# Two attentions on one core: attention two's query and key terms folded from SBUF to SBUF, norm and finish steps moved

## The chip, the core and the metric

The kernel runs on one core of a Trainium2 chip. The metric is the device time of one execution in microseconds; the profiled execution also has a span, from its first to its last instruction. Engines: TensorE (PE, with PEld for its weight loads), VectorE (DVE), ScalarE (ACT), GpSimd (POOL), and SyncE (SP), which here only issues transfers.

## The reference

x is (4, 16, 16, 256), that is four images of 256 tokens with 256 channels.

```
x = x + attention_one(group_norm(x))     # 8 heads of 16, relative bias, per image 8 x 256 x 256 scores
x = x + attention_two(group_norm(x))     # chunks of 64 tokens attend to their own and the previous chunk
attention_two: q, k, v = split(flat @ w_qkv.T)       # 16 heads of 16
               scores[h, l, m] = (q . k) * scale, over 128 keys; the first chunk has only its own 64
               out = softmax(scores) v, then @ w_out.T
group_norm: 32 groups of 8 channels, over all tokens of an image
```

All of it is float32. The kernel splits each float32 operand into a high float32r part and the low rest, and multiplies high by high, low by high and high by low.

## The kernel before

The work is eight units: units 0 to 3 are attention one of the four images, units 4 to 7 attention two of them (b = unit - 4). Each unit has eight blocks, and the whole is one row of steps t = 0 to 75 (`STEPS`), written out by hand for every engine: step t makes the scores of block t (unit t // 8), and the rest of the work is hung on steps by offsets from the unit's first block. `due(t, when, units)` is true for unit i at t = 8i + `when`. Each engine runs its own program in order and waits on semaphores, so where a step stands decides what it is queued behind.

In step t TensorE makes the scores of block t (`scores_b`, L590, in attention two: four matmuls of 96 rows), then transposes block t - 4 into the bank `z` (`shifted`, L600 and L609). VectorE takes the row maxima (L962, L958 in attention one) and subtracts them (L969; in attention one GpSimd, L362) into SB. ScalarE takes the exponential PT of the transposed block (`probabilities`, L1197). Scores of a block wait for the subtraction of two blocks before, transposes for that of their own block (four before) and for the PT of two before them.

Attention two, for each unit, with the offsets of before:

- XT (-14): TensorE transposes the image's X1 into bank F (L529), VectorE takes its statistics (L920, L925). Group mean (GM, -13): L538, which waits for the statistics and for bank G, that is for Qst (L881) or for ScalarE's copy VB (L1156) of the unit before. Group variance (GV, -12): L541, then VectorE's small steps, GpSimd's power (L376), and in the step after ScalarE's XTh and XT (L1133, two activations each) and after that GpSimd's XTl (L370).
- Queries and keys (QK, -9): L556, 24 matmuls; 8 on XTh and 8 more on XTh for the second bank once XT is out of it, then 8 on XTl. ScalarE copies the high parts to QHL and KHL (L1140, L1145), in the step after VectorE makes the low parts (L891). QHL and KHL are [128, 2 (high, low), 512].
- Values (V, -7): L567, which waits for VectorE's query terms; in the step after ScalarE copies them to VB (L1156), then GpSimd spreads them.
- Query and key terms: the 128 partitions of QHL are four pairs of heads by 32 rows. `scores_b` wants them as 96 partitions: 32 rows by three terms (high, low, high for queries; high, high, low for keys), with the four pairs side by side, in Q3 and K3. SP brings them there through DRAM: `put_terms` (L290) four stores of 128 KB for queries and four for keys, then `get_terms` waits for their landing and loads 512 KB into 64 partitions (L295) and 256 KB into 32 (L296). ScalarE masks the queries into QP (`pair_queries`, L1188, two activations at each even step, two steps ahead). All this stands on SP ahead of the stores of y (L316).
- Finish, per half of a unit (`FINISH`): the values matmuls (pv: 10 and 13, L679), ScalarE's copy OS (L1204, same step), the transposes t1 (12 and 15, L699), VectorE's reciprocal RC (L978) and ON (L986), the transposes t2 (14 and 17, L706), ScalarE's OT (L1212), the output product (16 and 19, L716), and in the step after VectorE's Y with the residual (L1001). The values matmuls of a half write the bank that the output product of the same half of the unit before used, so they wait for that Y.

Attention one has its own offsets (`TIMES_A`): L479 and ScalarE's XRh and VectorE's XRl, keys L494, value transposes L501, queries L485. VectorE copies the values out of bank G to VA (`value_rows`, L912) in the step after their transposes, behind that step's row maxima, and L485, which writes bank G, waits for it.

The weights of attention two are transposed by TensorE (L733) at steps 4, 5, 7 and 9, for queries, keys, values and output; ScalarE copies them to WTh (L1103), and VectorE makes WTl (L904). In steps 4 and 5 the same engines centre and scale the first images.

## Time and profile before

| | us |
|---|---|
| median of three runs | 173.7 |
| the three runs | 172.42, 173.70, 179.64 |
| the profiled execution, its own time | 175.27 |
| its span | 173.4 |
| TensorE busy in it | 151.1 |
| mean granted TensorE clock in it | 0.98 of 2.4 GHz |

The profiled execution is one execution; what is read from its rows is compared with its own time, 175.27 us, of which 1.9 us lie outside its span. In the rows, "idle before <- X" and "A <- B" give the time that an engine waited and what released it. L numbers are lines of the kernel before.

### The profile page before, as it was taken

Reading aid. Unit: us, or ns where it says so; the run is one execution under the profiler, and the core shown is the slowest. Engines: PE = TensorE matmul, PEld = TensorE weight load, DVE = VectorE, ACT = ScalarE, POOL = GpSimd, SP = SyncE. Lnnn points to the kernel's source line nnn. Section 1 sums busy time; section 2 is a strip of 40 time slices with the busy share of each in tenths; the row PEclk is TensorE's granted clock in tenths of the full one; section 3 lists DMA queues with packets and bytes.
Section 4 is the critical chain, followed back from the end, with each engine's and each line's share of the span. In section 5 each row is a group of like instructions: output and inputs, shape, how many; then the busy total and the mean of one; then the engine's idle time right before and its main releaser. Section 6 shows DMA issues by size and latency. Waiting matters only on the chain.

```text
span 173.4 us, 4284 instructions
## 1 busy us (share of the span) xinstructions
PE 151.1 (87%) x1582; PEld 130.9 (75%) x1582; DVE 111.1 (64%) x326; ACT 107.9 (62%) x218; POOL 53.0 (31%) x106
## 2 busy tenths in 40 slices
PE   7989769849989879999999798999999869989872
PEld 7568649737778578988797678988989758879751
DVE  1544776774366586277629887799687983898220
ACT  1427516857558457946795769775986774856520
POOL 0302540859946225762781122012200200000000
PEclk9999879999999999999999999999999996999999
DMA  6409900000000000049804990199309860100111
GB/s 184 138 4 275 325 6 4 0 0 0 6 2 0 4 0 2 0 121 242 246 4 104 233 266 6 32 243 240 102 5 259 206 202 0 34 14 17 34 55 42
DMA packets 8564, 15.84 MB, mean 91 GB/s; under 512 B 1208, under 2 KB 5688, under 8 KB 7776
## 3 DMA queue, kind: packets, MB, share of 16 engines
q1 hardware_dynamic: 7984, 15.22, 31.8%
q10 hardware_dynamic: 560, 0.35, 0.8%
q8 instruction: 13, 0.21, 0.5%
q14 instruction: 7, 0.06, 0.1%
HBM read 10.31 MB, written 5.26 MB: 90 GB/s over the span
## 4 chain that ended last, share of the span: by engine, by line
PE 64%; DVE 14%; DMA 6%; issue 6%; ACT 5%; POOL 2%; ACTq 1%; SPq 0%; DVEq 0%
PE bank L556 7%; PE bank L590 7%; PE bank L578 6%; PE bank L609 6%; PE bank L669 5%; PE bank L600 4%; PE bank L679 4%; PE bank L716 4%; PE bank L567 4%; DMA K<-k_terms 3%; PE bank L479 3%; DMA PT<-buckets 3%; DVE NM L962 2%; PE bank L712 2%; DVE SB L958 2%
## 5 line engine op out<-in xcount | busy, mean ns | idle before, releaser
L1197 ACT ACTIVATE PT<-bank 128x512 f32<-128x512 f32 x64 | 38.3, 598 | 23.0 <-PE bank L609 12.4
L958 DVE CUSTOM_DVE_ANT_0 SB<-bank,Tk 128x256 f32<-128x256 f32 x64 | 24.4, 420 | 20.6 <-PE bank L578 20.5
L362 POOL TENSOR_SCALAR SB<-SB,NM 128x256 f32<-128x256 f32 x64 | 29.9, 482 | 12.1 <-DVE NM L958 11.7
L962 DVE TENSOR_REDUCE NM<-bank 128x4 f32<-128x512 f32 x32 | 21.9, 685 | 12.7 <-PE bank L590 12.4
L590 PE MATMUL bank<-K,QP 96*128 96x128 f32 x128 | 21.8, 294 | 1.7 <-DMA K<-k_terms 1.7
L969 DVE TENSOR_TENSOR SB<-bank,NM 128x512 f32<-128x512 f32 x32 | 22.1, 692 | 1.1
L578 PE MATMUL bank<-KH,QM 128*128 128x256 f32 x64 | 20.6, 343 | 2.1 <-ACT QM L1177 2.1
L1188 ACT ACTIVATE QP<-Q,con 96x512 fp32r<-96x512 f32 x32 | 21.2, 713 | 0.0
L590 PEld LDWEIGHTS bank<-K,QP 96*128 96x128 f32 x128 | 17.8, 197 | 3.7 <-DMA K<-k_terms 2.0
L609 PE MATMUL bank<-con,SB 128*128 128x128 f32 x128 | 20.4, 283 | 0.0
L600 PE MATMUL bank<-con,SB 128*128 128x128 f32 x128 | 19.3, 273 | 0.0
L578 PE MATMUL bank<-KL,QM 128*128 128x256 f32 x64 | 17.3, 291 | 0.0
L578 PEld LDWEIGHTS bank<-KH,QM 128*128 128x128 f32 x64 | 12.6, 197 | 5.4 <-issue 4.9
L1177 ACT ACTIVATE QM<-Qst,con 128x256 fp32r<-128x256 f32 x32 | 16.0, 505 | 0.5 <-DVE Qst L881 0.5
L600 PEld LDWEIGHTS bank<-con,SB 128*128 128x128 f32 x128 | 14.6, 140 | 0.0
L609 PEld LDWEIGHTS bank<-con,SB 128*128 128x128 f32 x128 | 13.9, 143 | 0.2
L1204 ACT ACTIVATE OS<-bank 128x256 f32<-128x256 f32 (+1 forms) x16 | 7.8, 488 | 8.2 <-PE bank L669 5.3
L578 PEld LDWEIGHTS bank<-KL,QM 128*128 128x128 f32 x64 | 12.8, 199 | 0.2
L385 POOL COPY VB<-VB 64x256 f32<-64x256 f32 x4 | 1.6, 389 | 29.7 <-ACT VB L1156 29.7
L679 PE MATMUL bank<-PT,VB 128*32 128x64 f32 x512 | 8.8, 220 | 2.0 <-DVE Y L1001 2.0
L679 PEld LDWEIGHTS bank<-PT,VB 128*32 128x32 f32 x512 | 7.6, 110 | 3.5 <-issue 3.5
L716 PE MATMUL bank<-WoT,OT 128*128 128x256 f32 x32 | 9.3, 416 | 0.5 <-ACT OT L1212 0.5
(142 smaller groups left out, 269.7 us busy)
## 6 DMA issues: line engine op xcount, KB each, us to landing
q_terms<-WQK SPq DMA_DIRECT2D x16, 128.0 KB, 2.3
k_terms<-KHL SPq DMA_DIRECT2D x16, 128.0 KB, 2.4
Q<-q_terms SPq DMA_DIRECT2D x4, 512.0 KB, 5.4
K<-k_terms SPq DMA_DIRECT2D x4, 512.0 KB, 5.2
Tk<-bias_rows SPq DMA_DIRECT2D x4, 384.0 KB, 4.8
X<-x SPq DMA_DIRECT2D x4, 256.0 KB, 4.2
Q<-q_terms SPq DMA_DIRECT2D x4, 256.0 KB, 5.8
K<-k_terms SPq DMA_DIRECT2D x4, 256.0 KB, 6.1
```

What stands on the lines that cost most here:

```text
L362: last = nc.gpsimd.tensor_scalar(rows_of, rows_of, -1.0, NM[:, i % 2, 2 * u + nt:2 * u + nt + 1], ALU.mult, ALU.add)
L578: last = nc.tensor.matmul(s[:, nt * CH:(nt + 1) * CH], queries[:, nt * P:(nt + 1) * P], keys[:, i % 2, u // 4, :], start=(nt == 0 and keys ...
L590: last = nc.tensor.matmul(bank[S_BANK + u % 2][:, a * P:(a + 1) * P], QP[0:ROWS, c % QRING, a, g].rearrange("p v n -> p (v n)"), window, s ...
L600: last = nc.tensor.transpose(z[:, s * CH + nt * P:s * CH + (nt + 1) * P], below[:, nt * CH + s * P:nt * CH + (s + 1) * P], ident)
L609: last = nc.tensor.transpose(z[:, a * P:(a + 1) * P], below[:, a * P:(a + 1) * P], ident)
L679: last = nc.tensor.matmul(o[32 * hh:32 * hh + 32, col:col + CHUNK], VB[:, (i - BATCH) % 3, 2 * half + c2, h, :], PT[:, 4 * half + 2 * c2 + ...
L716: last = nc.tensor.matmul(o[:, 0:CH], OT[:, half, g, :], WoT[:, g, :], start=(g == 0), stop=(g == 1))
L958: last = V.tensor_tensor_reduce(SB[:, idx % SRING, nt * CH:(nt + 1) * CH], half, Tk[:, u, nt * P:nt * P + CH], 1.0, LOWEST, ALU.add, ALU.m ...
L962: V.tensor_reduce(NM[:, i % 2, 4 * u:4 * u + 4], s[:].rearrange("p (h m) -> p h m", h=4), AX.X, ALU.max).then_inc(max_ready, 1)
L969: V.tensor_tensor(SB[:, idx % SRING, :].rearrange("p (h m) -> p h m", h=4), bank[S_BANK + u % 2][:].rearrange("p (h m) -> p h m", h=4), NM ...
L1188: last = A.activation(QP[0:ROWS, c % QRING, :, :, v, :].rearrange("p a g n -> p (a g) n"), Q3[0:ROWS, b % 2, :, :, c * CHUNK:(c + 1) * CHU ...
L1197: A.activation(PT[:, u, :], bank[Z_BANK + u % 2][:], ACT.Exp, scale=-SCALE if is_a(i) else SCALE).then_inc(p_ready, 1)
```

## The change

It has five parts.

1. Terms: the DRAM tensors q_terms and k_terms and the semaphores q_written and k_written are gone. `fold_terms` takes each of the three terms of queries and keys from 128 partitions of QHL or KHL to 32 partitions of Q3 or K3 in one transfer of 256 KB, six a unit. Source partition 4r + a goes to target partition r, place a. ScalarE waits for q_loaded and k_loaded before it writes QHL and KHL again.
2. Weights: so that source partition 4r + a holds row r of pair a, the query and key weights are written in that order of columns: for n < 2 ScalarE's WTh and VectorE's WTl are written by two instructions each (one for each k), whose elements lie four apart.
3. Norm and projection steps of attention two: GM -13 to -12, GV -12 to -11, QK -9 to -8, V -7 to -6, with what follows them on the other engines; XT stays at -14.
4. Finish of attention two: t1, t2 and output product a step earlier for units 4 to 6; t1 and t2 a step earlier for unit 7.
5. VectorE's copy VA of attention one: in the step of its transposes, behind the query and key terms, instead of in the step after, ahead of them.

```diff
-        q_terms = nc.dram_tensor("q_terms", (BATCH, 2, GRP, PAIRS, 2 * TOK), F32, kind="Internal").ap()
-        k_terms = nc.dram_tensor("k_terms", (BATCH, 2, GRP, PAIRS, 2 * TOK), F32, kind="Internal").ap()
         rows = nc.dram_tensor("bias_rows", (HA, NDIAG), F32, kind="Internal").ap()
...
         fills, dve_fills = sem("fills"), sem("dve_fills")
-        q_written, k_written, q_loaded, k_loaded = (sem(n) for n in ("q_written", "k_written", "q_loaded", "k_loaded"))
+        q_loaded, k_loaded = sem("q_loaded"), sem("k_loaded")
         spread_ready = sem("spread_ready")
...
+        def pair_columns(w, n, k):
+            return w[:, k, n * CH:(n + 1) * CH].rearrange("p (g r a) -> p g a r", g=2, a=PAIRS)
+
         def grouped(t, b):
...
         TIMES_A = [(range(1, 2), (-6, -4, -5, -5)), (range(2, 3), (-5, -3, -4, -4)), (range(3, BATCH), (-9, -7, -8, -8))]
-        XT_B, GM_B, GV_B, QK_B, V_B = -14, -13, -12, -9, -7
+        XT_B, GM_B, GV_B, QK_B, V_B = -14, -12, -11, -8, -6
         FINISH = [(IN_A, (9, 12), (13, 13), (14, 14), (16, 16)),
-                  (range(BATCH, UNITS - 1), (10, 13), (12, 15), (14, 17), (16, 19)),
-                  (range(UNITS - 1, UNITS), (10, 13), (12, 15), (13, 16), (14, 17))]
+                  (range(BATCH, UNITS - 1), (10, 13), (11, 14), (13, 16), (15, 18)),
+                  (range(UNITS - 1, UNITS), (10, 13), (11, 14), (12, 15), (14, 17))]
...
-            def put_terms(b, terms, hl, ready, written):
-
-                sp.wait_ge(ready, BATCH + b + 1)
-                for a in range(PAIRS):
-                    sp.dma_start(terms[b, :, :, a, :].rearrange("s p n -> p s n"), hl[a * GRP:(a + 1) * GRP].bitcast(F32)).then_inc(written, 16)
-
-            def get_terms(b, terms, dst, both, high, written, loaded):
-
-                sp.wait_ge(written, 16 * PAIRS * (b + 1))
-                sp.dma_start(dst[GRP * both:GRP * (both + 2)], terms[b].rearrange("s p a n -> (s p) (a n)")).then_inc(loaded, 16)
-                sp.dma_start(dst[GRP * high:GRP * (high + 1)], terms[b, 0].rearrange("p a n -> p (a n)")).then_inc(loaded, 16)
+            def fold_terms(b, hl, parts, dst, loaded):
+
+                for s, part in enumerate(parts):
+                    sp.dma_start(dst[GRP * s:GRP * (s + 1), b % 2].rearrange("p a g n -> p a (g n)").bitcast(F32),
+                                 hl[:, part, :].bitcast(F32)).then_inc(loaded, 16)
...
-                n, i = b % 2, BATCH + b
-                put_terms(b, q_terms, QHL, q_ready, q_written)
-                put_terms(b, k_terms, KHL, k_ready, k_written)
+                i = BATCH + b
+                sp.wait_ge(q_ready, i + 1)
                 if b >= 2:
                     sp.wait_ge(qp_ready, NCH * (b - 1))
-                get_terms(b, q_terms, Q3[:, n].rearrange("p a g n -> p (a g n)"), 0, 2, q_written, q_loaded)
+                fold_terms(b, QHL, (0, 1, 0), Q3, q_loaded)
+                sp.wait_ge(k_ready, i + 1)
                 if b >= 2:
                     sp.wait_ge(s_done, BLK * (i - 1))
-                get_terms(b, k_terms, K3[:, n].rearrange("p a g n -> p (a g n)").bitcast(F32), 1, 0, k_written, k_loaded)
+                fold_terms(b, KHL, (0, 0, 1), K3, k_loaded)
...
                 elif u == 0:
-                    pe.wait_ge(k_loaded, 32 * (i - BATCH + 1))
+                    pe.wait_ge(k_loaded, 16 * TERMS * (i - BATCH + 1))
                 if not is_a(i) and u % 2 == 0:
...
                 src = bank[O_BANK][:].rearrange("p (k r) -> p k r", k=2)
-                V.tensor_tensor(WTl[:, :, n * CH:(n + 1) * CH], src, WTh[:, :, n * CH:(n + 1) * CH].bitcast(F32),
-                                op=ALU.subtract).then_inc(wl_ready, 1)
+                if n < 2:
+                    for k in range(CT):
+                        last = V.tensor_tensor(pair_columns(WTl, n, k), src[:, k].rearrange("p (g a r) -> p g a r", g=2, a=PAIRS),
+                                               pair_columns(WTh, n, k).bitcast(F32), op=ALU.subtract)
+                else:
+                    last = V.tensor_tensor(WTl[:, :, n * CH:(n + 1) * CH], src, WTh[:, :, n * CH:(n + 1) * CH].bitcast(F32), op=ALU.subtract)
+                last.then_inc(wl_ready, 1)
...
                     norm_x(2, t - 6)
-                for units, when in TIMES_A:
-                    for i in due(t, when[3] + 1, units):
-                        value_rows(i)
                 for step, when in enumerate((XT_B, GM_B, GV_B, GV_B + 1)):
...
                             queries_keys(i, which)
+                for units, when in TIMES_A:
+                    for i in due(t, when[3], units):
+                        value_rows(i)
                 for units, pv, t1, t2, out_step in FINISH:
...
                 src = bank[O_BANK][:].rearrange("p (k r) -> p k r", k=2)
-                dst = WTh[:, :, n * CH:(n + 1) * CH] if n < 3 else WoT[:]
-                A.activation(dst, src, ACT.Copy).then_inc(wb_ready, 1)
+                if n < 2:
+                    for k in range(CT):
+                        last = A.activation(pair_columns(WTh, n, k), src[:, k].rearrange("p (g a r) -> p g a r", g=2, a=PAIRS), ACT.Copy)
+                else:
+                    last = A.activation(WTh[:, :, n * CH:(n + 1) * CH] if n == 2 else WoT[:], src, ACT.Copy)
+                last.then_inc(wb_ready, 1)
...
                         if b:
-                            act.wait_ge(q_written, 16 * PAIRS * b)
+                            act.wait_ge(q_loaded, 16 * TERMS * b)
                         A.activation(QHL[:, 0, :], f[:], ACT.Copy).then_inc(qh_ready, 1)
...
                         if b:
-                            act.wait_ge(k_written, 16 * PAIRS * b)
+                            act.wait_ge(k_loaded, 16 * TERMS * b)
                         A.activation(KHL[:, 0, :], f[:], ACT.Copy).then_inc(kh_ready, 1)
...
                 if c == 0:
-                    act.wait_ge(q_loaded, 32 * (b + 1))
+                    act.wait_ge(q_loaded, 16 * TERMS * (b + 1))
                 if b * NCH + c >= QRING:
```

## Rows read from the trace of the kernel before

**Rows 1.** The page, part 1: busy time of each engine.

```profile
PE 151.1 (87%) x1582; PEld 130.9 (75%) x1582; DVE 111.1 (64%) x326; ACT 107.9 (62%) x218; POOL 53.0 (31%) x106
```

**Rows 2.** Windows by stage: length, busy time (instructions) of PE, PEld, DVE, ACT, POOL, clock, DMA share, GB/s.

```profile
50.00:87.00 37.00, 34.76 (x305) 30.33 (x304) 23.30 (x105) 24.68 (x54) 17.85 (x36) 1.00 0.27 72
87.00:158.00 71.00, 65.02 (x858) 59.07 (x856) 54.69 (x110) 52.01 (x101) 11.56 (x20) 0.98 0.46 120
```

**Rows 3.** Who waited for whom, PE's own: us in total, times, longest.

```profile
PE bank L679 <- DVE Y L1001: 2.0, 3, 0.8
...
PE bank L590 <- DMA K<-k_terms: 1.7, 1, 1.7
...
PE bank L485 <- DVE VA L912: 1.7, 3, 0.8
...
PE bank L538 <- ACT VB L1156: 1.6, 2, 1.2
...
PE bank L538 <- DVE Qst L881: 0.9, 1, 0.9
```

**Rows 4.** Timeline of units 6 and 7: start, us, engine, line.

```profile
128.43 0.68 DVE L891 TENSOR_TENSOR WQK<-bank,WQK 128x512 fp32r<-128x512 f32 x1
...
137.11 0.58 SPq L296 DMA_DIRECT2D K<-k_terms  x1
...
137.74 11.66 SPq L316 DMA_DIRECT2D y<-Y  x3
...
140.91 0.60 PE L699 MATMUL bank<-con,OS 128*128 128x128 f32 x4
```

**Rows 5.** The chain of waits, in order of time: start, us, what.

```profile
133.56 0.46 PE bank L609 x4
134.02 0.87 PE bank L716 x4
134.89 0.40 PE bank L590 x4
...
143.22 1.12 PE bank L590 x4
144.34 0.87 PE bank L609 x4
145.22 1.64 PE bank L716 x4
```

**Rows 6.** Windows around the wait for the key terms.

```profile
142.50:143.00 0.50, 0.00 (x0) 0.00 (x0) 0.43 (x1) 0.10 (x1) 0.00 (x0) 1.00 0.19 51
143.50:144.00 0.50, 0.50 (x4) 0.50 (x4) 0.00 (x0) 0.00 (x0) 0.00 (x0) 0.50 0.00 0
```

**Rows 7.** Windows of the stores, of the keys' load, of all unit 7's traffic.

```profile
112.00:116.00 4.00, 4.00 (x90) 3.54 (x89) 3.90 (x9) 2.13 (x5) 0.00 (x0) 1.00 0.94 249
119.50:121.00 1.50, 1.50 (x69) 1.24 (x68) 1.43 (x4) 0.64 (x2) 0.69 (x1) 1.00 0.85 224
...
129.50:142.50 13.00, 11.21 (x204) 10.31 (x202) 11.02 (x20) 9.22 (x19) 1.18 (x3) 1.00 0.86 222
```

**Rows 8.** The page, part 6: DMA issues, KB each, median us to landing.

```profile
q_terms<-WQK SPq DMA_DIRECT2D x16, 128.0 KB, 2.3
```

**Rows 9.** Timeline of the weights' step, and of two copies of 256 columns.

```profile
30.48 0.60 ACT L1103 ACTIVATE WTh<-bank 128x512 fp32r<-128x512 f32 x1 [0.43 <-PE bank L733]
...
115.59 0.64 ACT L1156 ACTIVATE VB<-bank 128x256 f32<-128x256 f32 x2
```

**Rows 10.** Timeline of ScalarE, GpSimd and PE around unit 7's projection.

```profile
122.33 1.02 ACT L1133 ACTIVATE Sq<-bank,gnb,grs 128x256 f32<-128x256 f32 x2
...
123.43 1.29 POOL L370 TENSOR_TENSOR XTl<-Sq,XTh 128x512 fp32r<-128x512 f32 x1 [3.19 <-ACT Sq L1133]
...
124.18 1.34 ACT L1188 ACTIVATE QP<-Q,con 96x512 fp32r<-96x512 f32 x2
...
124.78 1.22 PE L556 MATMUL bank<-XTl,WTh 128*128 128x256 f32 x8
```

## The prediction

> **What bounds the kernel now.** I read the page's busy times, then windows by stage, then who waited for whom on TensorE, then the timeline and the chain around the longest wait. TensorE is busy 151.1 of 173.4 us, against 111.1 for VectorE and 107.9 for ScalarE [rows 1]. By stages it is busy 34.8 of 37 us from 50 to 87, the end of attention one, and 65.0 of 71 from 87 to 158, attention two [rows 2]. There the time is TensorE's work plus its few waits, and a change is worth the waits that it takes off TensorE. They are [rows 3]: 2.0 us in three waits of the values matmuls (L679) for the output sum Y (L1001); 1.7 in one wait for the key terms; 1.7 in three waits of the query projection (L485) for the copy VA (L912); 1.6 and 0.9 in three waits of the group mean (L538) for VB (L1156) and for Qst (L881).
>
> The wait for the key terms costs more than it lasts. VectorE has the query terms at 128.43 + 0.68 = 129.1, the last load of the keys is issued at 137.11 [rows 4], and unit 7's first scores start at 143.22 [rows 5]. TensorE does nothing from 142.5 to 143, and at 143.5 the granted clock is 0.50, after 1.00 before it [rows 6]: 1.2 instead of 2.4 GHz. On the chain the three pieces behind the wait take 1.12 + 0.87 + 1.64 = 3.63 us, where the same three took 0.40 + 0.46 + 0.87 = 1.73 a unit earlier [rows 5]: 1.9 us of slow clock, and with the wait 3.6 us in all.
>
> **1. The transfers.** Removed, in each unit of attention two: eight 128 KB stores, SP's wait until they have landed, and loads of 768 KB each for queries and keys. Added: six folds of 256 KB. Bytes moved fall from 2,560 to 1,536 KB, and one flight takes the place of two. Issuing costs SP some 6 x 0.58 = 3.5 us (the load that fills 32 partitions [rows 4]), less than the data need, so it hides. No row shows a transfer within SBUF. The nearest: 249 GB/s over the stores in 2 KB pieces, 224 in the first part of the keys' load, 222 over all traffic of unit 7 [rows 7]. I take 220, with 170 and 300 as ends: 1.57 MB in 7.1 us (5.2 to 9.3). From issue to first bytes, and from the last ones to the semaphore, I estimate 0.8 us each, out of the 2.3 us in which 128 KB land [rows 8]. So the keys are there 8.7 us after the query terms (6.8 to 10.9), where now it takes 143.2 - 129.1 = 14.1.
>
> The projection that feeds the folds moves one step later, and the step that it skips holds one group of scores (0.40) and one of transposes (0.46) [rows 5] and little else. I put the query terms 1.2 us later, at 130.3 on the old clock. Unit 7's scores could have started when TensorE ran dry, at 140.91 + 0.60 = 141.5 [rows 4]. The room is 11.2 us, less 0.8 for a Y wait in between that goes: 10.4. So 8.7 fits, and 10.9 is late by 0.5. I count 3.0 of the 3.6 us as gained (0 to 3.6); some may come back because VectorE and ScalarE then follow closer. The query terms land some 5 us after they are ready and are wanted two steps before the keys, so they fit. Units 4 to 6 have more room. QHL and KHL are now held until their fold has landed, but the next unit writes them a whole unit later, so ScalarE's new waits cost nothing. On SP the stores of y stand behind all terms: the first went out at 137.74 [rows 4] and will go near 134; what waits for it, VectorE's Y of unit 5, comes some ten microseconds after.
>
> The Trainium skill speaks against such folds. SBUF — State Buffer, "Door 1: The DMA port swizzle", has it that partitions 0 to 31, and 0 to 63 no more, reach 8 of the 16 ports, 189 and 196 GB/s for 1 MiB against 328 for 128 partitions, and each fold writes 32. By that rule 1.57 MB would be an estimate of 8.3 us. The trace is a little kinder: it moved 224 GB/s while the load into 64 partitions ran [rows 7].
>
> **2. Finish steps one earlier (t1, t2, output).** The output sum of a half comes a step earlier, and the values that wait for it stay. Each of the three Y waits lasted at most 0.8 us [rows 3], less than a step. I take 1.6 of 2.0 gained (0.8 to 2.0). What is late next: t1 now stands one step behind the values and needs ScalarE's OS copy. A copy of 512 columns takes 0.60 [rows 9] and a start, some 0.7 in all; TensorE has 0.86 of scores and transposes before. In the tail there are no scores, the last transposes take 0.46, and the output product that lay between is now ahead of the values: 0.3 us lost (0 to 0.5).
>
> **3. Norm steps one later (group mean and variance, projections).** The group mean no longer stands right behind Qst, and VB falls into a step in which ScalarE has no QP: of the 2.5 us of waits [rows 3] I take 2.0 (1.0 to 2.5). The price is ScalarE's: XTh and XT (four activations, 1.02 a pair) fall from an odd step into an even one, where QP (1.34) stands ahead of them [rows 10]. Between the transposes of that step and its want of XTl TensorE has t1 (0.60 with its drain [rows 4], 0.44 without), a step with an output product (0.86 + 0.87 [rows 5]), scores and transposes (0.86) and the 16 matmuls of the projection on XTh (the last 8 took 1.22 with their drain [rows 10], so about 1.9): 4.9 us. ScalarE and GpSimd need about 0.5 for PT, 1.3 for QP, 1.8 for XTh and XT, whose pairs overlap a little, and 1.3 for XTl: 4.9, and starts. A tie, as it is today: XTl ends at 123.43 + 1.29 = 124.72, and the matmuls on it start at 124.78 [rows 10]. I add 0.15 in each of three units, 0.45 (0 to 1.5).
>
> **4. VA copied in the step of its transposes.** VectorE has 23.3 us of work in 37 there [rows 2], and the next block's scores stand behind the transposes on TensorE, so waiting in that step delays nothing that isn't late anyway. The query projection loses its wait: 1.7 us in three, 0.8 the longest [rows 3]; 1.4 gained (0.8 to 1.7).
>
> **5. Query and key weights written in pair order.** On ScalarE and on VectorE two instructions of 256 columns take the place of one of 512, twice each. WTh (0.60 [rows 9]) stands ahead of a PT and a QM for which TensorE waits, so this is on the path. Two copies of 256 columns take 0.64 together [rows 9], 0.04 more; four such pairs, 0.1 to 0.3. No row shows a write that leaves 16 bytes from element to element. At half speed it would be 0.3 more for each of four pairs, up to 1.2. I take 0.3 (0.1 to 1.2).
>
> **The sum.** 3.0 + 1.6 + 2.0 + 1.4 - 0.3 - 0.45 - 0.3 = 6.95 us. The profiled execution took 175.27 us (span 173.4), so 168.3. It lies 1.6 above the median of the runs, 173.7, and the load of the keys may be part of what differs between runs, so I carry 5.7 over to the median: **168.0 us**.
>
> **The rivals.** *A: the waits come back elsewhere.* VectorE has 54.7 and ScalarE 52.0 us of work in 71 [rows 2], in steps too uneven to hide behind a TensorE that never waits. Then the waits for XTl, for the query terms before the value projection, and for VectorE in steps without other work take half of terms 2 and 3 (1.8) and 1.4 of term 1: 168.0 + 3.2 = 171.2. For it: ScalarE's full step [rows 10]. Against: scores run two blocks ahead and transposes have four to spare. 0.20. That only the load's wait goes and the moved orders do nothing (173.7 - 3.0 = 170.7) is a milder form of it.
>
> *B: gapped writes are slow.* Term 5 at its upper end, 1.2 for 0.3, and as much as 0.6 behind it, since Mu and the centring on GpSimd follow WTl on VectorE: 168.0 + 0.9 + 0.6 = 169.5. 0.12. The Trainium skill has the mechanism: by SBUF — State Buffer, "Door 1: The DMA port swizzle", lines are 16 bytes long and every access that crosses to a new one pays. No run here shows it.
>
> *C: slower, because the folds crawl.* If 32 target partitions hold a fold back, the keys come late in each unit. In unit 7 data have 10.4 - 1.6 = 8.8 us, so the wait comes back below 180 GB/s; the others have, by the same count, 12.2 to 13.0, so below 130. From 150 GB/s down (10.5 us: 1.7 late, 1.9 of slow clock, and the 3.0 of term 1 not gained) it is slower than before: 174.6. At 120 GB/s 13.1 us pass, 4.3 late and 1.7 over the other units: 168.0 + 3.0 + 6.0 + 1.9 = 178.9. For it: nothing of the kind was measured. Against: 224 GB/s into 64 partitions [rows 7]. 0.08.
>
> **How the numbers follow.** Forecast 0.60, A 0.20, B 0.12, C 0.08. Two per cent, about what can be told from no change, is 170.2 and 177.2. Below lie nearly all of the forecast, most of B and little of A: 0.66. Above lies most of C: 0.07. Between: 0.27. The forecast's own range is 165 to 170.5; with A and the mild part of C, 164.5 to 173.5.
>
> **What would show it.** Right: L590 waits for no transfer and the clock stays at 1.00 from 143 on; the keys land 8 to 10 us after the query terms; waits for Y, VA, VB and Qst are under 0.3 us each; TensorE is busy over 95% of attention two. Wrong by step: L590 waits for K (term 1, C); L556 waits over 0.5 us for XTl (A); two writes of WTh take over 1 us (B); L699 waits over 0.5 us for OS in the tail. If those waits go and the span does not fall, the chain was not TensorE's.

## The result, and the profile after

The changed kernel takes 201.57 us (median of 4 runs, 200.14 to 202.82), the kernel before 175.45 us beside it (172.42 to 179.64, 4 runs): the ratio is 1.165 (95% interval 1.147 to 1.182). The prediction said 168.0 us. The profiled execution took 200.14 us, its span 198.3. Executions of one kernel come in a shorter and a longer kind (for the kernel before 172.42 and 173.70 us against 177.21 and 179.64 here); medians are those of all runs, while each ratio, and with it each "faster" or "slower" below, compares the shorter kind alone, of which the kernel before had one to three beside most experiments, so a ratio is not the quotient of the medians beside it.

From the page: busy times, the clock over 40 slices, and the new transfers of the keys with their median us to landing:

```profile
PE 162.1 (82%) x1582; PEld 140.7 (71%) x1582; DVE 112.3 (57%) x328; ACT 109.7 (55%) x220; POOL 53.0 (27%) x106
...
PEclk9955699999999999985999859699579995899999
...
K<-KHL SPq DMA_DIRECT2D x12, 256.0 KB, 10.2
```

Terms no longer pass through DRAM. But TensorE is busy 11.0 us longer than in [rows 1] over the same 1582 matmuls, and in the second half the clock falls once in each unit of attention two, and in unit 5 a second time, for 3.4 us from 125.8, behind the wait for X.

Who waited for whom on TensorE, first from 50 to 90 us, then from 90 to 180 (us in total, times, longest):

```profile
PE bank L585 <- DMA K<-KHL: 3.5, 1, 3.5
```

```profile
PE bank L585 <- issue: 7.8, 2, 4.1
PE bank L585 <- DMA K<-KHL: 3.7, 1, 3.7
PE bank L524 <- DVE X L995: 2.8, 2, 2.0
```

Gone from [rows 3] are the waits for Y, VA and Qst; of the 1.6 us for VB 1.3 are left (L533, L538 before). New are four long waits at the scores (L585, L590 before), of two kinds, and 2.8 us of L524 (L529 before) for the residual sum X. The first kind is late keys. The chain ahead of unit 4's first scores (start, us, what):

```profile
73.44 0.61 DVE WQK L886
...
76.71 0.61 SPq L290
...
77.36 11.34 DMA K<-KHL
...
88.75 1.11 PE bank L585 x4
...
90.73 4.81 PE bank L551 x24
```

and windows of the folds (the wait is in it) and of what follows (length; busy time of PE, PEld, DVE, ACT, POOL; clock, DMA share, GB/s):

```profile
86.00:87.00 1.00, 0.00 (x0) 0.00 (x0) 0.00 (x0) 1.00 (x3) 0.00 (x0) 1.00 1.12 127
...
90.00:92.00 2.00, 2.00 (x11) 2.00 (x10) 1.28 (x2) 1.23 (x3) 0.82 (x2) 0.50 0.04 8
```

The query terms are ready at 73.44 + 0.61 = 74.05, and the last fold of the keys, 11.34 us after its issue at 77.36, has landed at 88.70: 14.65 us. All DMA engines are busy (share 1.12) and move 127 GB/s; six folds of 262 KB need 12.4 us at that rate. TensorE ran dry at 85.24, at the end of attention one, and waited 3.5 us; then the granted clock is 0.50, 1.2 GHz, and the 24 matmuls of the projection, right behind, take 4.81 us. Unit 5 is the same.

The second kind, ahead of units 6 and 7, has no releaser ("issue"). The chain at the longer one, and the DMA queues from 124.5 to 136.4 us, then from 136.4 to 139 (packets, MB, share of 16 engines):

```profile
135.30 0.26 PE bank L585
135.56 4.10 issue
139.66 0.69 PE bank L585 x3
```

```profile
q1 hardware_dynamic: 852, 1.56, 107.1%
```

```profile
q8 instruction: 1, 0.02, 4.2%
```

This isn't a unit's first group of scores but the one two blocks ahead, and TensorE stops after one of its four matmuls, where the program has no wait. Queue 8 carries TensorE's own program: 13 packets and 0.21 MB over the span, 16 KB each. From 124.5 to 136.4, while the folds run, none of its packets does; one starts at 136.5, when they are done, and takes until 138.3 (its share of 16 engines, 4.2% of 2.6 us, is 1.7 us), and TensorE goes on at 139.66, 1.4 us behind its end. The other stop is alike, but here the folds are still running when the packet comes: it takes from 161.0 to 162.7, and TensorE goes on at 164.47. In the kernel before, two such packets passed in 12 us of its stores and loads:

```profile
q1 hardware_dynamic: 896, 2.62, 81.5%
q8 instruction: 2, 0.03, 1.0%
```

By the Trainium skill (Runtime: NRT & Kernel Launch, "Instruction fetch mechanics") each engine's program comes in blocks of 16 KiB, 256 instructions, over a DMA queue of its own. The packets here agree in their size. The page has the cost of a new block mostly hidden; here it was 7.8 us of standing still, as e12 to e16 show.

**The account.** From where TensorE ran dry in unit 4 to the last block's first row maximum:

```profile
85.20:183.50 98.30, 77.35 (x864) 70.36 (x864) 55.24 (x112) 53.92 (x104) 10.96 (x19) 0.84 0.44 57
```

98.3 us for 864 matmul records, against 71.0 for 858 in [rows 2]. Of the 27.3 us, 12.3 are longer busy time, 7.2 late keys (3.5 + 3.7) and 7.8 the stops without a releaser; the waits lost and won elsewhere are about even. The whole profiled execution is 24.9 us longer than the one before (200.14 against 175.27), as the parts ahead of and behind this stretch are 2.4 us shorter.

### The profile page after: what moved, and what is told of

It is laid out like the page before. It is cut to its first block, busy times and chain, and to the rows that moved or that the text cites. A ratio compares the mean times of both kernels' runs of the same rounds, so it can differ in the third digit from the quotient of the medians.

```text
span 198.3 us, 4264 instructions
## 1 busy us (share of the span) xinstructions
PE 162.1 (82%) x1582; PEld 140.7 (71%) x1582; DVE 112.3 (57%) x328; ACT 109.7 (55%) x220; POOL 53.0 (27%) x106
## 4 chain that ended last, share of the span: by engine, by line
PE 60%; DMA 11%; DVE 10%; issue 8%; ACT 4%; SPq 3%; POOL 2%; DVEq 0%
DMA K<-KHL 11%; PE bank L551 8%; PE bank L585 7%; PE bank L604 7%; PE bank L573 5%; PE bank L674 5%; PE bank L711 5%; PE bank L595 3%; SPq L290 3%; PE bank L694 2%; DVE Part L792 2%; PE bank L733 2%; PE bank L664 2%; PE bank L562 2%; PE bank L707 2%
## 5 line engine op out<-in xcount | busy, mean ns | idle before, releaser
L585 PE MATMUL bank<-K,QP 96*128 96x128 f32 x128 | 24.6, 318 | 15.8 <-issue 7.8
L585 PEld LDWEIGHTS bank<-K,QP 96*128 96x128 f32 x128 | 20.1, 219 | 18.7 <-issue 8.6
L573 PE MATMUL bank<-KH,QM 128*128 128x256 f32 x64 | 21.3, 352 | 2.3 <-ACT QM L1181 2.2
L604 PE MATMUL bank<-con,SB 128*128 128x128 f32 x128 | 22.3, 302 | 0.1
L595 PE MATMUL bank<-con,SB 128*128 128x128 f32 x128 | 19.7, 277 | 0.0
L573 PE MATMUL bank<-KL,QM 128*128 128x256 f32 x64 | 17.8, 298 | 0.0
L573 PEld LDWEIGHTS bank<-KH,QM 128*128 128x128 f32 x64 | 13.1, 204 | 6.0 <-issue 5.0
L604 PEld LDWEIGHTS bank<-con,SB 128*128 128x128 f32 x128 | 15.2, 154 | 0.5 <-DVE SB L969 0.3
L595 PEld LDWEIGHTS bank<-con,SB 128*128 128x128 f32 x128 | 14.9, 142 | 0.0
L711 PE MATMUL bank<-WoT,OT 128*128 128x256 f32 x32 | 10.2, 449 | 0.5 <-ACT OT L1216 0.5
L674 PE MATMUL bank<-PT,VB 128*32 128x64 f32 x512 | 9.6, 232 | 0.0
L674 PEld LDWEIGHTS bank<-PT,VB 128*32 128x32 f32 x512 | 8.3, 118 | 1.9 <-issue 1.2
```

Of the source, the lines that this page charges most:

```text
L573: last = nc.tensor.matmul(s[:, nt * CH:(nt + 1) * CH], queries[:, nt * P:(nt + 1) * P], keys[:, i % 2, u // 4, :], start=(nt == 0 and keys ...
L585: last = nc.tensor.matmul(bank[S_BANK + u % 2][:, a * P:(a + 1) * P], QP[0:ROWS, c % QRING, a, g].rearrange("p v n -> p (v n)"), window, s ...
L595: last = nc.tensor.transpose(z[:, s * CH + nt * P:s * CH + (nt + 1) * P], below[:, nt * CH + s * P:nt * CH + (s + 1) * P], ident)
L604: last = nc.tensor.transpose(z[:, a * P:(a + 1) * P], below[:, a * P:(a + 1) * P], ident)
L674: last = nc.tensor.matmul(o[32 * hh:32 * hh + 32, col:col + CHUNK], VB[:, (i - BATCH) % 3, 2 * half + c2, h, :], PT[:, 4 * half + 2 * c2 + ...
L711: last = nc.tensor.matmul(o[:, 0:CH], OT[:, half, g, :], WoT[:, g, :], start=(g == 0), stop=(g == 1))
```

## The experiments

**e1: moves without folds.** The kernel before with the new offsets and the early VA copy.

```diff
-        XT_B, GM_B, GV_B, QK_B, V_B = -14, -13, -12, -9, -7
+        XT_B, GM_B, GV_B, QK_B, V_B = -14, -12, -11, -8, -6
...
-                  (range(BATCH, UNITS - 1), (10, 13), (12, 15), (14, 17), (16, 19)),
-                  (range(UNITS - 1, UNITS), (10, 13), (12, 15), (13, 16), (14, 17))]
+                  (range(BATCH, UNITS - 1), (10, 13), (11, 14), (13, 16), (15, 18)),
+                  (range(UNITS - 1, UNITS), (10, 13), (11, 14), (12, 15), (14, 17))]
...
-                for units, when in TIMES_A:
-                    for i in due(t, when[3] + 1, units):
-                        value_rows(i)
...
+                for units, when in TIMES_A:
+                    for i in due(t, when[3], units):
+                        value_rows(i)
```

> The kernel before with parts 3, 4 and 5 of the forecast's order of steps alone (norm and finish steps moved, VA copied earlier); terms still go through DRAM, weights in their old order. Theory 1 (the folds' transfer rate is the whole loss, the moved steps gain what the forecast said): 1.6 + 2.0 + 1.4 - 0.75 = 4.2 us faster than before, though the key terms of unit 7, asked for 1 us later, wait longer and may take 2 to 3 us of it back: 170 to 174 us. Theory 2 (the moved steps themselves lose): slower than before by 5 us or more.

Measured: 183.87 us (183.37 to 184.45) against 176.42; ratio 1.061 (1.047 to 1.074). The moves alone make the kernel slower. Its long waits on TensorE are 1.3 us once and 4.3 in two for K, and 2.8 of L529 for X.

**e2: folds without moves.** The changed kernel with all offsets and the VA copy of before.

> The kernel after with the old offsets and the old place of VA: only the folds and the weights' order are changed against before. Theory 1: 13 us for the six folds at about 123 GB/s make the keys late by some 2 to 4 us in every unit and slow the clock behind each: 192 to 202 us, a span close to the changed kernel's, keys landing about 13.5 us after the query terms. Theory 2: close to before, under 180 us.

Measured: 182.81 us (182.64 to 184.11); ratio 1.056 (1.042 to 1.070). There is no wait for keys at all. The longest idle time is of the second kind. Its chain, and the DMA queues from 122.9 to 123.4 us, while the folds run:

```profile
121.80 0.48 PE bank L585 x3
122.28 4.13 issue
126.41 0.26 PE bank L585
```

```profile
q1 hardware_dynamic: 40, 0.07, 104.6%
q8 instruction: 1, 0.02, 21.7%
```

It could be taken for late keys. The place (three of four matmuls done, two blocks ahead of the unit) says otherwise, and e12 to e16 test it. A packet of TensorE's program takes from 123.1 to 124.9 us, and TensorE goes on at 126.41. There is a second idle time of 2.0 us, ended at 149.10, which the view gives to the subtraction (SB) ahead of a group of transposes. Those transposes take a block of four steps before, so its SB was long done; a packet of queue 8 takes from 145.4 to 147.1, and this too is most likely a stop for code.

The moves alone (1.061) and the folds alone (1.056) would make 1.12 together, and the whole change has 1.165: some 8 us, uncertain by 4 or 5, arise only where both meet. The long late keys of units 4 and 5 do so too.

**e3: pair order through DRAM.** The changed kernel, with the terms taken through DRAM; the new order of the weights allows one store of 512 KB in place of four of 128.

```diff
-                fold_terms(b, QHL, (0, 1, 0), Q3, q_loaded)
+                sp.dma_start(terms[b].rearrange("s p a n -> (p a) s n"), hl[:].bitcast(F32)).then_inc(written, 16)
+                get_terms(b, q_terms, ...)
```

> The changed kernel with its moved steps and its order of weights, but the terms go through DRAM again: one store of 512 KB for queries and one for keys (the new order of columns makes one store enough), then the loads of before. Theory 1 (rate of the folds): stores and loads at 220 to 250 GB/s bring the keys 11 to 13 us after the query terms; 168 to 174 us, 27 to 33 us faster than the changed kernel. Theory 2 (steps or weights lose): above 180 us.

Measured: 178.56 us (176.82 to 180.74); ratio 1.027 (1.006 to 1.047). With everything else of the change in place, the way through DRAM is 23 us faster than the folds: keys land some 12 us after the query terms, and the waits for them sum to 1.9 us.

**e4: transfers by themselves.** Only transfers of 256 KB between tiles; x is copied to the output. Each group is issued together, and the next waits for it.

```diff
+            burst([(fold[32 * s:32 * s + 32], src[:]) for s in range(3)])
+            burst([(same[:, s], src[:]) for s in range(3)])
+            burst([(half[64 * (s % 2):64 * (s % 2) + 64], src[:]) for s in range(2)])
...
```

> No attention at all: only bursts of transfers of 256 KB, each burst waited for before the next, to measure rates; the output is a copy of x. Bursts in order: 128 to 32 partitions as in the change (fold); 128 to the same 128 partitions (same); 128 to 64 (half); 32 to 32 in rows of 8 KB (rows32); SBUF to DRAM (store); DRAM to 32 partitions in 2 KB pieces (from2k) and 8 KB rows (from8k); DRAM to 128 (from128); 32 to 32 partitions in 64 KB transfers (plain); fold in 1 KB pieces (short) and in 4 KB pieces (long4); 64 partitions exchanged with the other 64 (shift). Theory A (few target partitions are slow): fold, half, rows32, from2k, from8k at about 125 GB/s; same, from128 and shift at 220 or more. Theory B (SBUF to SBUF is slow whatever the shape): fold, same, half, shift all at about 125, from2k, from8k and store at 200 or more. Theory C (only crossing from a partition to a distant one is slow): same and rows32 at 220 or more, fold, half and shift at 125.

Measured, in windows of the fold, of 128 to 128 partitions, of 128 to 64, of the store to DRAM, of the load from DRAM into 32, of one fold by itself, and of the first 0.6 us of the three folds (length, POOL, clock, DMA share, GB/s):

```profile
8.00:11.00 3.00, 0.00 (x0) 1.00 1.08 128
...
16.40:17.40 1.00, 0.00 (x0) 1.00 1.03 389
...
20.00:22.00 2.00, 0.00 (x0) 1.00 1.08 131
...
31.00:32.00 1.00, 0.00 (x0) 1.00 1.00 375
35.00:37.00 2.00, 0.00 (x0) 1.00 1.04 229
...
58.50:59.90 1.40, 0.00 (x0) 1.00 0.88 187
7.40:8.00 0.60, 0.00 (x0) 1.00 1.21 345
```

The fold has its rate with nothing beside it. It isn't SBUF to SBUF as such (389), nor the piece of 2 KB, which the first four rows share. The load from DRAM into 32 partitions reaches 229, but in pieces of 8 KB, as the packets show, first of this load and then of the fold by itself:

```profile
DMA packets 144, 0.79 MB, mean 157 GB/s; under 512 B 48, under 2 KB 48, under 8 KB 48
DMA packets 144, 0.26 MB, mean 105 GB/s; under 512 B 16, under 2 KB 16, under 8 KB 144
```

So it can't tell whether 32 target partitions are slow in pieces of 2 KB; e11 can. The fold by itself was meant to go in pieces of 1 KB, but its 128 packets with data carry 2 KB like those of every fold, so pieces of 1 KB stay unmeasured. It shows that a fold with none behind it isn't that slow, 187 GB/s; and of the three in a row the first 0.6 us go at 345, and only what follows at 128. No rule stated ahead covers all rows.

**e5 and e10: VA alone.** The kernel before with only the last part of e1's diff.

> The kernel before with VA copied a step earlier, nothing else. The forecast's price was a gain of 1.4 us (0.8 to 1.7), under the 2% that can be told apart; the trace must show no wait of L485 for VA. Rival: the saved wait turns up in another one before unit 4, and nothing is gained.

> e5 again, beside e9 on the same chip: VA alone. 173 to 175 us, 1 to 4 us under before; the wait of L590 for K stays between 1 and 2 us.

Measured: 173.28 us (173.13 to 174.97, 4 runs) beside 177.78 (172.10 to 178.02, 7 runs), ratio 1.006, too few runs for an interval; again 173.90 us (173.01 to 177.61, 6 runs) beside 177.81, ratio 1.011 (1.003 to 1.018). The wait of L485 is gone, and the time is not less.

**e6: finish steps alone.** Of e1's diff only the lines of the finish steps.

> The kernel before with the finish steps moved, nothing else. The forecast: 1.6 - 0.3 = 1.3 us faster, no waits of L679 for Y. Rival: t1, right behind the values, waits for OS in every half, 0.3 us each, and nothing is gained.

Measured: 178.33 us (174.20 to 186.32) beside 177.78, ratio 1.016, without an interval: nothing is gained. The Y waits are gone; in their place stands one longer than all of them:

```profile
PE bank L699 <- ACT OS L1204: 2.5, 1, 2.5
```

At the old norm offsets ScalarE's XTh and XT fall into the step of the values matmuls and stand ahead of OS, for which t1 waits.

**e7: norm and projection steps alone.** Only the first two lines of e1's diff.

> The kernel before with the norm and projection steps of attention two moved, nothing else. Theory 1 (the room between query terms and first scores shrinks, not by the 1.2 us of the forecast but by a whole projection of the next unit besides, 2.9 us, so that keys through DRAM are late in each unit; and VectorE's sum X1 stands behind the wait for QHL in the same step): this part alone carries the loss of the moved steps, 183 to 187 us, with waits of L590 for K in most units and of L529 for X. Theory 2 (the finish steps lose): about the time of before.

Measured: 186.50 us (183.60 to 189.57) beside 177.78, ratio 1.070, without an interval: no less than all of e1 loses. VectorE around attention one's residual sum, of the kernel before and then of e7, with TensorE's next transposes:

```profile
111.14 0.68 DVE L891 TENSOR_TENSOR KHL<-bank,KHL 128x512 fp32r<-128x512 f32 x1
113.06 0.68 DVE L995 TENSOR_TENSOR X<-bank,X 128x512 f32<-128x512 f32 x1
```

```profile
117.40 0.68 DVE L891 TENSOR_TENSOR KHL<-bank,KHL 128x512 fp32r<-128x512 f32 x1
117.99 0.68 DVE L995 TENSOR_TENSOR X<-bank,X 128x512 f32<-128x512 f32 x1
...
118.73 0.70 PE L529 MATMUL bank<-con,X 128*128 128x128 f32 x4 [1.98 <-DVE X L995]
```

Before, L891 was a step ahead of L995. Moved by one it stands right ahead of it, and waits for ScalarE's copies of the projection: L529 waits 1.98 us. And the projection itself, which stood ahead of the unit's first scores, now stands behind them. e7 waits for keys in three units, 1.3 us once and 3.8 in two, though its transfers are those of before.

**e8: pair order, one store, finish and VA moved, norm steps of before.**

> Weights in pair order, one store of 512 KB each for queries and keys through DRAM, VA and finish steps moved, but norm steps at the offsets of before. If the room is what decides, keys 12.1 us after the query terms in place of 14.1 are in time in every unit: no wait of L590 for K, and 168 to 172 us, 4 us or more under before in the same call. If the weights' order or the finish steps lose, it is no faster than before.

Measured: 178.02 us (175.86 to 178.22) beside 177.78, ratio 1.034, without an interval: slower, where 4 us less were expected. The wait for keys falls to 0.3, and the wait for OS is back at 2.5, as in e6. The finish steps need the moved norm steps, and these bring e7's price.

**e9: pair order, one store and VA; norm and finish steps of before.**

> Norm and finish steps as before; VA a step earlier; weights in pair order; terms through DRAM with one store of 512 KB each for queries and keys. If the finish steps alone were what undid e8 (the one wait of L699 for OS, 2.5 us), keys 12.1 us after the query terms are in time in unit 7 too: no wait of L590 for K, against 1.4 us in e5; weights cost about 1 us early on. 171 to 174 us: 0 to 2 us under VA alone (e10 of this call), 3 to 6 under before. Rival: the weights' price eats the whole of it, and it is not under VA alone.

Measured: 173.80 us (171.42 to 176.02, 12 runs) beside 177.81 (171.99 to 182.44, 18 runs); ratio 1.001 (0.992 to 1.010). No wait for keys is left, and no gain can be measured. No version here beats the kernel before.

**e11: transfers by themselves, second set.** As e4, with other partitions read and written.

```diff
+            burst([(gap32[32 * s:32 * s + 32, :, 0:N], wide[:]...) for s in range(3)])
+            burst([(open128[:, s], wide[:]...) for s in range(3)])
+            burst([(low64[0:64, s], src[0:64]) for s in range(6)])
+            burst([(near32[0:32, s], src[0:64]) for s in range(6)])
...
```

> Bursts of transfers again, no attention, the output a copy of x. In order: fold (control, 127 GB/s expected again); gap32, 32 to 32 partitions in 2 KB pieces; gap128, 128 to 128 in 2 KB pieces with a gap; open128, 32 to 128 partitions (the fold turned round); low64, partitions 0-63 to 0-63; near32, 0-63 folded into 0-31; far32, 0-63 folded into 64-95; cross64, 64-127 to 0-63; quarter, 32-63 to 0-31; store; from2k, DRAM to 32 partitions. Theory X (a transfer within SBUF is slow when its source partitions and its target partitions are dealt out differently, 8 rows of source to 2 of target for an engine): fold, open128, near32, far32 near 130; gap32, gap128, low64, cross64, quarter at 200 and more. Theory Y (2 KB pieces into 32 partitions of SBUF from SBUF are slow): fold, gap32, near32, far32, quarter near 130 and open128 fast.

Measured, in windows of the fold, of 32 to 32 partitions in pieces of 2 KB, of 32 to 128 and of 64 to 64:

```profile
8.00:11.00 3.00, 0.00 (x0) 1.00 1.09 129
16.00:18.00 2.00, 0.00 (x0) 1.00 0.97 193
...
26.00:28.00 2.00, 0.00 (x0) 1.00 1.00 205
32.00:33.00 1.00, 0.00 (x0) 1.00 0.88 199
```

Both rules stated ahead fall. In pieces of 2 KB, 32 target partitions are not slow by themselves (193 from 32, 195 from 64). Of all that was measured only what leaves all 128 partitions for 32 (129) or for 64 (131 in e4) is this slow. Why stays open.

**e12, e13, e14: the same programs, shifted.** e2's kernel with 128 and with 64 more instructions at the start of TensorE's program, and the changed kernel with 128.

```diff
             pe.wait_ge(dve_fills, 1)
+            for n in range(128):
+                pe.wait_ge(dve_fills, 1)
```

> e2's kernel with 128 more instructions at the start of TensorE's program, where it is idle (waits on a semaphore long past); nothing else differs. Code theory: TensorE's 4.1 us of 'issue' in e2 is its own code, loaded 16 KB at a time through the same DMA engines as the folds and held behind the folds already queued; 128 instructions are half a load, so the loads of attention two come some 3 to 5 us earlier in the program, and the idle time is at another place of the program or differs in length by over 1 us. Data theory: those matmuls wait for something in the data (keys, masked queries) whose releaser the trace doesn't name; the program's place in memory means nothing to it, so 4.1 +/- 0.3 us stands again within the group of scores two blocks ahead of unit 6's first.

> As e12 with 64 instructions, a quarter of a load. Code theory: the place differs from both e2's and e12's, or the length does by over 1 us. Data theory: 4.1 +/- 0.3 us at e2's place.

> The changed kernel with the 128 instructions of e12. Code theory: the two idle times without a releaser (4.1 us ahead of unit 6, 3.7 ahead of unit 7) are at other places or of other lengths, and the waits for K at the first scores of units 4 and 5 (3.5 and 3.7) stay within 0.5, being the data's. Data theory: all four stay as they are, 201 +/- 1 us.

Measured: 190.25, 188.37 and 197.97 us (2 runs each) beside 176.00 (3 runs), ratios 1.088, 1.089 and 1.145, without intervals. TensorE's long waits of e12, of e13 and of e14:

```profile
PE bank L735 <- issue: 8.0, 1, 8.0
PE bank L674 <- issue: 5.5, 2, 2.8
```

```profile
PE bank L735 <- issue: 4.5, 1, 4.5
PE bank L674 <- issue: 6.9, 2, 4.5
```

```profile
PE bank L585 <- DMA K<-KHL: 10.4, 3, 3.8
```

L735 is TensorE's first work, behind the added instructions. Nothing that these programs compute differs from e2 and from the changed kernel, and the stops move from the scores to the values matmuls (L674), or vanish. The stretch ahead of the first stop, of the changed kernel, of e2, of e13 and of e12 (length, TensorE's busy time and matmuls, and so on), and the stretch between the two stops, of the changed kernel and of e2:

```profile
0.00:135.60 135.60, 113.78 (x929) 98.11 (x930) 79.56 (x267) 78.11 (x161) 50.33 (x102) 0.89 0.38 65
0.00:122.30 122.30, 108.39 (x929) 92.84 (x930) 79.22 (x268) 77.32 (x159) 50.73 (x102) 0.93 0.40 70
0.00:123.95 123.95, 106.21 (x914) 90.70 (x914) 78.66 (x267) 77.29 (x159) 50.73 (x102) 0.94 0.39 69
0.00:125.75 125.75, 104.53 (x898) 89.46 (x898) 78.42 (x266) 77.13 (x159) 50.50 (x102) 0.96 0.38 67
```

```profile
139.60:160.80 21.20, 20.32 (x249) 18.81 (x248) 13.28 (x24) 13.98 (x28) 2.45 (x4) 0.84 0.38 49
126.40:147.10 20.70, 19.74 (x249) 18.49 (x248) 13.90 (x24) 12.61 (x24) 1.19 (x3) 0.87 0.49 62
```

TensorE stops after 929 matmuls in the changed kernel and in e2, though their steps stand in another order, after 914 with 64 instructions more, and after 898 with 128. From one stop to the next it is 248 or 249 in all four, e2's second idle time included. So the places are those of the program in memory, not of its data: these are loads of code. (A matmul and its weight load are two instructions, so 128 more should move the place by some 64 matmuls and not by 31; why it is half stays open.) Each of the eight stops ends 1.4 to 2.0 us after a packet of queue 8 has ended: e12's at 127.1 and 150.4, where TensorE goes on at 128.56 and 152.07, and e13's at 127.1 and 149.9, where it goes on at 128.41 and 151.62.

The 128 instructions weren't free: unit 4's query terms are ready at 79.5 in e14, 5.5 us later than in the changed kernel, and e14 is still 3.6 us faster. So the two stops cost the changed kernel, as an estimate, some 9 us more than the third late key that e14 has in their place.

**e15: one fold at a time.** e2's kernel; SP waits for the landing of each fold before the next.

```diff
                 for s, part in enumerate(parts):
+                    if s:
+                        sp.wait_ge(loaded, 16 * (TERMS * b + s))
...
+                sp.wait_ge(q_loaded, 16 * TERMS * (b + 1))
                 fold_terms(b, KHL, (0, 0, 1), K3, k_loaded)
```

> e2's kernel, but SP issues each fold only when the one before has landed, so that no more than one (2 us) is queued ahead of a load of code. Code theory: no idle time of TensorE without a releaser is over 0.5 us. Six folds one after another take 6 x (2.1 + 1.5) = 22 us in place of 14.7, so the keys are late in all units, named as a wait for K, and the kernel is slower than e2's 182.8, near 200. Data theory: idle time without a releaser remains, and is longer than in e2.

Measured: 216.91 us (2 runs) beside 176.00, ratio 1.254, without an interval. No stop without a releaser is left, and L588 (the scores) waits 29.4 us for K in four units: a fold takes 3.9 us from issue to landing, six of them 24. That is 17 us slower than expected.

**e16: two bursts.** e2's kernel with the VA copy moved; the keys' folds are issued when the queries' have landed.

```diff
+                sp.wait_ge(q_loaded, 16 * TERMS * (b + 1))
                 fold_terms(b, KHL, (0, 0, 1), K3, k_loaded)
```

> The folds at the old offsets (e2) with the VA copy moved (e5), and SP issues the three folds of the keys only when the three of the queries have landed. At most three folds (6.2 us) are ever queued ahead of a load of TensorE's code, and a load can pass in the gap between the two bursts. Code theory: the 4.1 us without a releaser fall below 1.5. The keys come 1.5 to 2 us later than e2's 14.7 after the query terms, about 16.5, against a room of about 15, so each unit waits for K by 0.5 to 2 us; in all about as fast as e2 or up to 5 us faster, 178 to 183 us, still slower than before. Rival (traffic theory: a code load suffers from any fold in flight, queued up or not): the idle time without a releaser stays at 3 us or more.

Measured: 180.97 us (180.16 to 185.82) against 177.14; ratio 1.021 (1.013 to 1.029). The ratio is too kind to e16: the kernel before, run beside it, had no run under 176.04, while beside the other experiments its best were 172 to 173, and against 172.5 e16 stands near 1.046. No stop without a releaser, keys late by 7.0 us in three units. So it is the queue of six folds that holds the code up, not a fold in flight. It need not run empty: the packet that ended a stop came when the folds had run for 7.5 us (five times), 9.6 (twice) or 12.0 (once), steps of about one fold, and 5.4 in e16, near the end of three. When TensorE asked for a block no view shows. At this rate, in the orders tried, the keys were in time or the code was, not both.

## Why the prediction was wrong

**Term 1, the rate: "I take 220, with 170 and 300 as ends".** It is 127, with six queued. The ends came from transfers with DRAM on one side, and none of them bounds a fold. With 12.4 us in place of 7.1 my own sum gives 14.0 us; 14.65 was measured, 8.7 predicted. Rival C had this and its threshold, and 0.08: its counter-evidence, 224 GB/s into 64 partitions, was a load from DRAM. What the Trainium skill gives for 32 partitions (SBUF — State Buffer, "Door 1: The DMA port swizzle": 189 GB/s) lies near 193 from 32 to 32 in e11 and below 229 from DRAM in e4; it isn't that of queued folds.

**Term 1, what was left out: TensorE's code.** I had the folds compete only with themselves. They hold the DMA engines for 12 us, and TensorE's program has to come meanwhile: 4.1 us in e2 and most likely 2.0 more, 7.8 in the changed kernel, each with slow clock behind. In no term and no rival; shown by e12 to e16.

**"Units 4 to 6 have more room."** I moved the projection for the folds' start and didn't follow it to the other end. Its 24 matmuls stood ahead of the next unit's scores and now stand behind, so TensorE gets there sooner: unit 4's room was 85.24 - 74.05 = 11.2 us, not 12.2 to 13.0. e2, at the old offsets, has the same folds and no late key; e7, with the old transfers, has three.

**The clock.** C counted 1.9 us of slow clock once. Each of the four long waits brought it, in unit 4 right ahead of the projection: 4.81 us for 24 matmuls that took 2.87 at unit 6's first step, at full clock. The wait for X brought it once more. In all TensorE was busy 12.3 us longer.

**Term 3, norm steps (+2.0).** Qst's wait went, VB's did not: 1.3 of its 1.6 us are left, where the sign of being right was under 0.3 for each. And I asked only for ScalarE's and GpSimd's queue and not for VectorE's, where L891 came to stand ahead of L995: 2.8 us, in e1, e3, e7 and the changed kernel alike. The tie for XTl held. Alone (e7) the term is no gain of 2.0 but a loss of about 12 (ratio 1.070).

**Term 2, finish steps (+1.6).** The Y waits went, as said; that this hangs on term 3 (e6, e8) I didn't see.

**Term 4, VA (+1.4).** The wait went and the time didn't (e5, e10). Where it came back I didn't settle. In e5's profile the projection at the end of attention one starts 1.1 us earlier than before (85.98 against 87.10) and the next one at the same 105.66; between them the granted clock is 0.50 from 100 to 103, where it was 1.00.

**Term 5, gapped writes (0.3, at most 1.2).** The timeline of the changed kernel's weights:

```profile
26.95 1.11 ACT L1104 ACTIVATE WTh<-bank 128x256 fp32r<-128x256 f32 x2 [1.15 <-PE bank L728]
28.09 1.15 DVE L901 TENSOR_TENSOR WTl<-bank,WTh 128x256 fp32r<-128x256 f32 x2 [1.42 <-ACT WTh L1104]
29.30 0.66 PE L728 MATMUL bank<-con,VB 128*128 128x128 f32 x4 [0.77 <-DVE WTl L901]
```

A pair takes 1.11 us where two ungapped copies took 0.64 [rows 9]: about 0.5 for each of four pairs, and a wait of 0.8 on TensorE. So gapped writes are slow, as rival B has it; what they cost the whole, 1.5 us by B, no run isolates.

**Right** were that a unit's wait for keys costs its length and the slow clock behind it, that issuing hides, and that the waits for Y, VA and Qst go. That was worth a few us against 27. The sign of the whole was wrong, and none of the parts that were run alone is a gain.

## What to carry to other kernels

Measure transfers of a new shape by themselves, as many in a row as the kernel queues, before a schedule is built on them, and count what else comes through the DMA engines while it is queued, the engines' own programs too: an idle time without a releaser, in the middle of a group that waits for nothing, is the sign. When a step is moved, list for every engine what it now stands ahead of and what it no longer does; filler ahead of a wait is room for a transfer. Price a TensorE wait with the work right behind it.

## What was not expected of the hardware

- Several transfers in a row out of 128 partitions into 32 or 64 within SBUF: 127 to 131 GB/s with all DMA engines busy, against 389 for 128 into 128 and 193 to 205 for 32 into 32, 32 into 128 and 64 into 64. The first 0.6 us went at 345, and a fold with none behind it at 187.
- A 16 KB load of TensorE's code came only after three to six of six queued folds (7.5 to 12.0 us), and TensorE stood up to 4.5 us for it; no such stop stood beside the stores and loads of before.
- 128 more waits on a semaphore at the start of TensorE's program moved its first matmul from 1.05 to 7.95 us (e12), and 5.5 us of that were left at unit 4 (e14).
- A fold of 256 KB takes SP 0.55 to 0.65 us to issue, e3's store of 512 KB 0.38.
